# Eight fixed products fewer at the end of the fused stage, eight more in the pauses of attention's last batch

## The reference

```
x = x + tanh(g_xattn[0]) * xattn(layernorm(x), ctx_768, Wq, Wk, Wv, Wout, bout)   # 8 heads of 64, 77 keys
x = x + tanh(g_ffn[0]) * ffn(layernorm(x), Wg, W1, W2, Ws1, Ws2)
# ffn: scores = softmax(xf @ Wg.T); top 2 of 16 experts, weighted
#      z = sum over the two of w * (u * silu(g)) @ W2[e], with u, g = split(xf @ W1[e])
#      ys = gated(xf @ Ws1) @ Ws2;  out = z + ys
```

## Time and profile before

| | |
|---|---|
| median of 3 timed runs | 984.84 us (982.47 to 984.85) |
| profiled execution | 979.39 us |
| its span, first to last instruction | 977.6 us |
| mean granted TensorE clock | 0.972 of full speed |
| PE busy | 916.9 us, 94% of the span |
| DVE busy | 812.9 us, 83% |

### The profile page before, as it was taken

The page is one execution under the profiler, slowest core; times in us unless marked ns, Lnnn a source line. Parts: engine busy times, 40 slices in busy tenths (PEclk is TensorE's granted clock), DMA queues, the critical chain, the costliest instruction groups (busy, mean ns, idle before and its releaser), DMA issues. The chain is left out here.

```text
span 977.6 us, 20907 instructions
## 1 busy us (share of the span) xinstructions
PE 916.9 (94%) x6722; PEld 851.2 (87%) x6722; DVE 812.9 (83%) x1928; ACT 524.2 (54%) x1191; POOL 495.2 (51%) x605
## 2 busy tenths in 40 slices
PE   6699999999999999999879999999689999899996
PEld 5599999999999999998758888888569999699996
DVE  6899999999999999988758888888728877378885
ACT  6477776777777776554355444554114444144442
POOL 4445355354635435444433555555506766546776
PEclk8799999999999999999979999999889999999998
DMA  8213223322331333454262444442358999488882
GB/s 241 75 47 107 73 67 107 93 73 82 107 92 51 104 94 122 116 159 145 98 197 76 171 169 171 166 163 104 120 190 282 355 329 336 135 283 262 271 275 78
DMA packets 108342, 151.14 MB, mean 155 GB/s; under 512 B 21831, under 2 KB 72395, under 8 KB 108241
## 3 DMA queue, kind: packets, MB, share of 16 engines
q1 hardware_dynamic: 92880, 107.60, 36.0%
q0 software_dynamic: 15360, 42.24, 11.3%
HBM read 90.19 MB, written 65.90 MB: 160 GB/s over the span
## 5 line engine op out<-in xcount | busy, mean ns | idle before, releaser
L681 POOL TENSOR_TENSOR prob<-prob,row_sum 128x616 f32<-128x616 f32 x64 | 77.9, 1217 | 141.3 <-DVE row_sum L903 141.3
L1124 POOL DMA_INDIRECT rows_scratch<-row,slot x64 | 67.8, 1060 | 74.9 <-DVE row L1377 60.3
L1530 POOL DMA_INDIRECT rows_scratch<-prow x80 | 78.7, 984 | 52.3 <-issue 30.7
L1530 POOL DMA_INDIRECT out<-prow x80 | 78.7, 983 | 49.3 <-issue 28.0
L1640 ACT ACTIVATE eyT_hi<-ps_ey 128x512 fp32r<-128x512 f32 x80 | 47.9, 598 | 99.8 <-PE ps_ey L1552 98.4
L75 PE MATMUL ps_h<-w_flat,eyT_hi 128*128 x320 | 96.8, 302 | 0.0
L76 PE MATMUL ps_h<-w_flat,eyT_hi 128*128 x320 | 90.0, 281 | 0.0
L77 PE MATMUL ps_h<-w_flat,eyT_lo 128*128 x320 | 89.9, 281 | 0.0
L1684 DVE TENSOR_TENSOR eyT_lo<-ps_ey,eyT_hi 128x512 fp32r<-128x512 f32 x80 | 55.3, 692 | 40.6 <-ACT eyT_hi L1640 37.5
L75 PE MATMUL ps_s<-M_hi,xT_hi 128*128 128x308 f32 x256 | 81.5, 318 | 7.6 <-PEq L387 4.9
L815 ACT ACTIVATE prob<-prob,rstd 128x616 f32<-128x616 f32 x64 | 51.9, 812 | 66.6 <-DVE prob L893 66.6
(11 more groups left out here) (295 smaller groups left out, 3351.3 us busy)
## 6 DMA issues: line engine op xcount, KB each, us to landing
prow<-rows_scratch SPq DMA_DIRECT2D x160, 258.0 KB, 3.8
rows_scratch<-blank SPq DMA_DIRECT2D x34, 258.0 KB, 4.2
xT_raw<-in_xT SPq DMA_DIRECT2D x32, 256.0 KB, 4.5
x_tok<-in_x SPq DMA_DIRECT2D x32, 256.0 KB, 2.8
x_scratch<-x_tok SPq DMA_DIRECT2D x32, 256.0 KB, 3.1
row<-x_scratch SPq DMA_DIRECT2D x16, 512.0 KB, 3.9
x_ahead<-in_x SPq DMA_DIRECT2D x26, 256.0 KB, 4.4
w_raw<-in_W SPq DMA_DIRECT2D x16, 256.0 KB, 3.5
```

The lines of the kernel that those rows point to most:

```text
L681: nc.gpsimd.tensor_tensor(pr, pr, row_sum[i][:, :].unsqueeze(2).broadcast_to((P, H, CK)), ALU.mult).then_inc(normed, 1)
L1124: pool.indirect_dma_start(c.rows1, bass.IndirectOffsetOnAxis(slot1[:, t:t + 1], 0), row[G % NX][:, i, :], None).then_inc(scattered[G % NX] ...
L1530: pool.indirect_dma_start(dram, bass.IndirectOffsetOnAxis(target, 0), row[u][:, i, 0:columns], None, bounds_check=bound, oob_is_err=False) ...
```

## The change

Five fixed products of 256 columns stand ahead of `attend_values(B - 1)`, and three ahead of `project_out(B - 1)`. They multiply by `bias` and write to `ps_proj[1]`, a bank that nothing in the last group of batches uses. At the end of `mix` three products of 384 columns are issued in place of eleven. No wait is added or removed.

```diff
                 groups(pe, body)
+                busy(nc, c, ps_proj[1], c.bias[:, :], 5)
                 attend_values(B - 1)
+                busy(nc, c, ps_proj[1], c.bias[:, :], 3)
                 project_out(B - 1)
...
                 last.then_inc(table_rows, 1)
-                busy(nc, c, ps_h[0], c.stats2[:, :], 11)
+                busy(nc, c, ps_h[0], c.stats2[:, :], 3)
```

## The result

The changed kernel took 972.85 us in the median of 4 runs (972.43 to 974.84), the kernel before 983.65 us in the same comparison (4 runs, 981.06 to 984.85): ratio 0.9894, 95% interval 0.9867 to 0.9922. Three later comparisons of the same two kernels gave 0.9926 (0.9899 to 0.9954), 0.9916 (0.9886 to 0.9945) and 0.9937 (0.9911 to 0.9963). The change saves 7.4 us, give or take 1, and the first comparison fell on the favourable side of that, which was luck.

What follows compares the result with a forecast made beforehand. At the end of `mix` PE's fixed products bound the block; in attention's last batch VectorE and ScalarE did. Savings 5.21 + 0 + 0 + 0.3 = 5.5 us, from 984.84 to 979.3 us, range 975 to 982.5.

Steps and rivals of the forecast that it cites:

- The end of `mix`: End of `mix`: PE's fixed products are what is waited for; three in place of eleven save 5.21 us.
- the room under it: End of `mix`: scatters land at about 709.8, 1.36 us before PE's shortened fixed products end at 711.16.
- The start of `passes`: Start of first pass: everything moves forward whole; low-clock stretch taken as 0, bounds -2.5 to +2.5 us.
- The last batch of `attend`: Attention's last batch: fixed products fit PE's pauses, delay 0 to +0.2 us; avoiding clock falls saves 0.3, between 0 and 5.8.
- the rival on that side: Attention's last batch: fixed products issued at clock 0.50 delay it by 3.0 us, saving 2.2, 982.6 us; chance 0.03.
- The sum against the profiled execution: Whole kernel: the profiled execution's 979.39 us less the 5.5 saved gives 973.9 us.

Runs made afterwards that it cites:

- The two profiles with none: No fixed product at the end of `mix`: the changed kernel without its three, 973.72 us; the same with more fixed products at the starts of `mix` and `passes`, 974.78 us.
- the two profiles of the longer pause: Kernel before plus four VectorE subtractions before the last value products: pause open, ratio 1.0059; filled with eleven fixed products, and three before the projection, 1.0028.

## Why the prediction fell short

**The end of `mix`: right.** PE's fixed products were what the block's end waited for, GpSimd's scatters had room, and all of it was on the path. 5.21 us were worked out, 5.22 measured between the first two profiles and 10.48 - 5.14 = 5.3 between the means of all. The two profiles with none show that the room under it, given as 1.36 us by the windows, was smaller: GpSimd's wait was shorter by 0.6 to 1.0 us than in most profiles with three. The prediction took the scatters' landing for the moment at which GpSimd is ready, and the run with none shows some 1.2 us from the landing to the next instruction, where 0.4 us pass once PE is the last.

**The start of `passes`: 0 as a sum, which the profiles can't contradict.** From the first transposes to the end of the program it is 256.6, 254.4, 255.5, 256.6, 254.3 and 254.9 us in the six profiles of the kernel before, and 254.5, 256.6, 252.5 and 257.3 in the four of the changed one: means of 255.4 and 255.2. The differences between executions of one kernel there, up to 4.8 us, are larger than the 2.5 us that the prediction gave the clock at the seam, so ten profiles can't tell 0 from 1 or 2 us.

**The last batch of `attend`: the mechanism was right, the size was the step that failed.** "I take 0.3 us, between 0 and 5.8, near the end that the trace shows" rested on one execution without a fall. The fall came in 3 of 8 profiles with open pauses and in none of 10 with the first one filled, and cost 1.5, 2.3 and 3.7 us in the tail. If filling had no effect, all three falls would be among the eight open ones with a chance of 7% (56 in 816); with the two profiles of the longer pause, four falls in 9 open against none in 11 filled, it is 3%. The falls average 7.5 / 8 = 0.9 us in the tail. The whole span points the same way: the three profiles of the kernel before with a fall have a mean of 980.2 us and the three without 978.0. The two timed kernels with attention alone changed saved 1.6 and 4.0 us, mean 2.8. In place of 0.3 the term is between 1 and 3 us, which lies inside the bounds of 0 to 5.8 that the prediction gave it. That the fixed products fit the pauses without delay (0 to 0.2 us was the bound) held to 0.01 us, and so the rival on that side didn't come about.

**The range: too narrow for a median of four.** "A median of three can move by some 2 us either way" was taken from three runs that lay 2.4 us apart. Over 105 runs the kernel before spreads from 978.0 to 987.9 us, the changed one over 24 from 971.9 to 978.6. The four runs of the first comparison had a mean of 973.2, 2 us below the mean of all 24. The base was off as well: 984.84 us, from three runs, is 2.2 us above the mean of the 105. So the forecast of 979.3 was 4.1 us above the changed kernel's mean of 975.2, 2.2 of them from the base and 1.9 from the saving, and the rest of the way to the measured 972.85 is the scatter of four runs. With this scatter about 975.2, a low end of 975.0 had no room beneath it. The sum against the profiled execution came nearer, 973.9 forecast and 973.07 measured, and neither that execution nor the changed kernel's had a fall in attention. With executions of one kernel several microseconds apart, a part of that is luck.

**What stays open.** The parts that the profiles show sum to 5.3 + 0.9, and some 0.2 us in `mix`: 6.4 us. The runs say 7.4, give or take 1. The 105 executions of the kernel before have a mean of 982.6, and the six profiled ones (five of them among the 105) one of 980.9. Whether the fall in attention is more frequent in the others can't be seen, since they left no trace.

## What to carry to other kernels

Fixed products that keep the clock belong where PE waits for another engine in the middle of its work, and no more of them than the pause holds at the full clock; at the end of a block, where the next dense work is some microseconds away, each one past the next slowest engine is paid in full (5.2 us for eight here). A pause of 2 us can be harmless in one profile and cost 1.5 to 3.7 us in the next, so take several profiles before you price the clock at nothing. And before a range is set by the spread of three runs, look at how the same kernel's executions differ: here their standard deviation was 2.4 us, and a base from three of them was 2.2 us off.

## What the runs showed of the hardware

The granted clock at one place of an unchanged program differed between executions, with pauses of the same length (2.11 or 2.12 us, and 1.41): it stayed at 1.00 in three profiles of the kernel before and in the two of other kernels with the same pauses, and was 0.50 for 3.4 to 10 us in the other three of the kernel before. The Trainium skill, TensorE: Matmul & The Clock Gate, Part 1, says that the number of matmuls at the low clock when a kernel starts varies from run to run; these runs show the like in the middle of a kernel. Fixed products cost up to twice as much when they are issued at the low level (6.07 us for ten instructions against 3.43, 2.85 for four against 1.50), so a filling that fits at the full clock can delay the work behind it at the low one. Two single executions, one with five products alone and one with the start of `mix` filled, took 2287 and 2282 us. Neither left a trace; the granted clock on record is 1.00 in both, so it wasn't the clock, and the cause stays open. The ratios above leave them out; without them the medians would be 979.6 and 975.99 us in place of 979.78 and 976.61.
